# Attention probabilities transposed by VectorE blocks and two DMAs instead of on TensorE, in a four-layer graph network on one core

## Chip, cores and metric

The kernel runs on one core of a Trainium2 chip. The metric is the device time of one execution in microseconds, the median of the timed runs.

## What is computed

The input `x` holds 32 samples of 256 tokens with 384 features, `adj` a 256x256 Boolean graph for each sample. Four residual layers follow one another, each closed by a LayerNorm. The first is a graph attention layer with 12 heads (GAT), which the change leaves alone. The other three are masked self-attention with 6 heads of 64 features:

```python
q = _heads(x @ Wq + bq); k = _heads(x @ Wk + bk); v = _heads(x @ Wv + bv)
scores = jnp.einsum('bhqd,bhkd->bhqk', q, k) / np.sqrt(HEAD_SIZE)
bias = jnp.where(adj, 0.0, -9e15)[:, None]
probs = jax.nn.softmax(scores + bias, axis=-1)
ctx = jnp.einsum('bhqk,bhkd->bhqd', probs, v)      # back to (token, 384)
x = _layernorm(x + ctx @ Wf + bf)
```

All of it is float32 in and out.

## The kernel before

The three attention layers have 96 samples to work through (32 in each), and do so as a software pipeline of slots. A function `slot(cur, nxt, prev, ...)` is written out for each engine. In one slot the engine works on three samples: `nxt` is projected (transposed x, then Q and K in three chunks, then V), `cur` gets its scores and softmax, and `prev` gets its contexts, its output projection ("back") and its LayerNorm. Nothing reorders this: each engine takes its instructions in the order in which its `slot` writes them, and semaphores join the engines. A sample is written `(half, u)`, and `before` and `after` use the same two halves of double buffers by `u`.

A product of two matrices is made of three matmuls (`product`, L78 to L80), with each operand split into a high and a low part in float32r. ScalarE makes the high part out of PSUM (`high_xt`, `high_qk`, `high_ct`), VectorE the low one (`low_xt`, `low_qk`, `low_ct`).

The softmax of a head goes this way. `pair_of_scores` writes the scores of heads 2c and 2c+1 (pair c, three pairs a sample) into the PSUM banks `s0` and `s1`. VectorE's `mask_and_max` (L1001) adds the mask and takes the maximum, ScalarE's `exp` (L727) takes the exponential and its sum, VectorE's `normalise` takes the reciprocal of the sums (L1019) and multiplies the probabilities by it (L1022). The tile `probs` has room for four heads, that is two pairs. TensorE's `pair_of_transposes` (L1411) then turns each 128x128 block of a head, eight blocks a pair, into the PSUM banks `pt0` and `pt1`; ScalarE copies the even head to SBUF (`even_pt`) and VectorE the odd one (`odd_pt`, L1009). The contexts (L1429) multiply V by the turned probabilities `pt_copy`.

GpSimd has the work around it: `make_mask` (L495), `add_output_bias` (L501), the inverse standard deviation (L506, L508) and the LayerNorm itself (L516), and in 12 slots of layers 1 and 2 one part of the next layer's weights split in two (L523, L525). SyncE issues every DMA, in one order: `move` (rows of Q and K to the other half of the partitions, two DMAs of 128 KB a chunk, `stack<-split`), the load of a later sample with its graph (448 KB) and the store of a finished one (384 KB). An instruction that waits on SyncE or GpSimd holds back everything written behind it.

The scratch banks in PSUM are two (`pj0`, `pj1`) for the projections, and one each (`cx`, `pj2`, `pj0`) for the three pairs of contexts.

Of the kernel before, what the change touches and what calls it, by code (L numbers as in the profile page):

```python
# [4 lines left out]
F32 = mybir.dt.float32  # L5
# [63 lines left out]

def held(eng, sem, value, passed):  # L70

    eng.wait_ge(sem, value)
    eng.sem_inc(passed, 1)
# [9 lines left out]
def network(nc, x, adj, gat_w, gat_sd, gat_b, gat_hb, att_w, att_b_col, att_b_row, ident_dram, sel_dram, y):  # L83


    g_STEPS, STEPS = 9, 7
# [3 lines left out]
    g_PT_BUFS, PT_BUFS = 2 * g_QUAD, 6  # L90
    Q, K, V, O = range(4)
    with ExitStack() as ctx:  # L92
# [60 lines left out]
        pt_sb = sb("pt_copy", [P, PT_BUFS, NT, N])  # L153
# [21 lines left out]
        w_lo.append(sb("w_lo1", [P, 4, DC, D], F32R))  # L175
        s_ps = [ctx.enter_context(nc.psum_tensor(f"s{i}", [P, NT, N], F32)) for i in range(2)]
# [3 lines left out]
        cx_banks = [cx_ps, pj_ps[2], pj_ps[0]]  # L180
# [30 lines left out]
        pj_made = sem("pj_made")  # L211
# [5 lines left out]
        inverted, normed = sem("inverted"), sem("normed")  # L217
        transposed = sem("transposed")
        pt_even_read, pt_odd_read = sem("pt_even_read"), sem("pt_odd_read")
        pt_read = [pt_even_read, pt_odd_read]  # L220
# [35 lines left out]
        X, QK, VS = (0, 1), (2, 4, 6), (3, 5)  # L256
        HI_STEPS = len(X) + len(QK)
        BANK_ORDER = ("x0", "x1", "ctx2", "qk0", "v0", "qk1", "v1", "qk2", "back0", "back1")

        def step(half, u, k):  # L260

            return at(STEPS, half, u, k + 1)
# [5 lines left out]
        def bank(u, what):  # L268


            return pj_ps[BANK_ORDER.index(what) % 2]

        def evictions(half, u, h):

            return at(HEADS // 2, half, u, h // 2 + 1)

        def pt_slot(u, h):
            return (HEADS * u + h) % PT_BUFS
# [30 lines left out]
        g_even, g_odd = (HALVES - 1, 0), (HALVES - 1, 1)  # L309

# [3 lines left out]
        def _(sp):  # L314
# [35 lines left out]

            def sample(half, u, stored_pair, loaded_pair):

                move(half, u, 0)
                if stored_pair is not None:
                    store(half - 2 + u, stored_pair, 1 - u)
                move(half, u, 1)
                move(half, u, 2)
                if loaded_pair is not None:
                    load_again(half, u, loaded_pair)
# [17 lines left out]
            start(sp, *g_stored, *stored, *moved)  # L377
# [35 lines left out]
            end = LAYERS * HALVES - 1  # L413
            store(end - 1, HALVES - 2, 1)
# [1161 lines left out]
```

## Time and profile before

| | us |
|---|---|
| median of 3 runs | 2952.93 |
| lowest and highest | 2952.66, 2953.56 |
| span of the profiled execution | 2950.5 |

| engine | busy us | share of the span | instructions |
|---|---|---|---|
| TensorE matmul | 2901.4 | 98% | 22432 |
| TensorE weight load | 2635.8 | 89% | 22432 |
| VectorE | 2593.1 | 88% | 8649 |
| ScalarE | 2428.1 | 82% | 6888 |
| GpSimd | 1269.5 | 43% | 1262 |

The profiled execution is 2.4 us shorter than the median. The GAT layer takes about the first 850 us of the span, the three attention layers the rest. Busy shares tell how full an engine is; what sets the time is read from who waits. Matmuls are pipelined, so the time of one is longer than the distance between two.

### The profile page before, as it was taken

The page shows a single profiled execution, that of the slowest core. Times are in us where ns is not written, and L with a number is a line of the kernel's source. Part 1 is how long each engine was busy: PE and PEld are TensorE (multiplying, and loading weights), DVE is VectorE, ACT ScalarE, POOL GpSimd, SP SyncE. Part 2 cuts the span into 40 slices and gives each one's busy share as a digit, 9 for nine tenths or more (in the row PEclk, how much of TensorE's full clock was granted, in tenths as well). Part 3 has the DMA queues.
Part 4 walks back from the last instruction along what each step waited for, and adds up shares of the span by engine and source line. Part 5 has one row for each costly group of instructions (what it writes and reads, how often), then busy time and mean ns, then how long its engine had stood idle before and what let it go on. Part 6 is the DMA issues. An engine that isn't in the chain of part 4 may idle for free. (4 is left out here: it accounts for less than half of the span.)

```text
span 2950.5 us, 72423 instructions
## 1 busy us (share of the span) xinstructions
PE 2901.4 (98%) x22432; PEld 2635.8 (89%) x22432; DVE 2593.1 (88%) x8649; ACT 2428.1 (82%) x6888; POOL 1269.5 (43%) x1262
## 2 busy tenths in 40 slices
PE   8999999999999999999999999999999999999998
PEld 7888888888889999999999999999999999999997
DVE  6999899999888888888888888888888888888887
ACT  7999999999987777777777777777777777777775
POOL 3777776766643343332332333433323323223233
PEclk9999999999999999999999999999999999999999
DMA  2111111010123222223223222222232222222321
GB/s 91 36 36 36 36 36 36 31 36 31 36 73 110 73 77 77 75 74 81 72 77 109 78 77 75 74 78 74 75 80 77 78 73 77 77 75 75 81 72 55
DMA packets 153211, 198.76 MB, mean 67 GB/s; under 512 B 48896, under 2 KB 115328, under 8 KB 152448
## 3 DMA queue, kind: packets, MB, share of 16 engines
q1 hardware_dynamic: 152832, 194.13, 24.0%
q8 instruction: 186, 3.05, 0.4%
q14 instruction: 193, 1.58, 0.2%
HBM read 68.24 MB, written 50.33 MB: 40 GB/s over the span
## 5 line engine op out<-in xcount | busy, mean ns | idle before, releaser
L501 POOL TENSOR_TENSOR residual<-x,br 128x384 f32<-128x384 f32 x192 | 189.6, 1008 | 1329.4 <-DVE mix L1031 1316.2
L727 ACT ACTIVATE probs<-logits,nmax 128x256 f32<-128x256 f32 x1152 | 574.0, 502 | 111.0 <-DVE nmax L1001 104.1
L78 PE MATMUL pj<-xt_hi,w_lo 128*128 128x256 f32 x1728 | 506.9, 293 | 0.0
L80 PE MATMUL pj<-xt_hi,w_hi 128*128 128x256 f32 x1728 | 480.9, 278 | 0.0
L79 PE MATMUL pj<-xt_lo,w_hi 128*128 128x256 f32 x1728 | 480.8, 278 | 0.0
L1001 DVE CUSTOM_DVE_ANT_0 logits<-s,mask 128x256 f32<-128x256 f32 x1152 | 432.5, 419 | 5.8
L1022 DVE TENSOR_SCALAR probs<-probs,recs 128x256 f32<-128x256 f32 x1152 | 398.3, 387 | 20.4
L598 ACT ACTIVATE g_exps<-g_v,g_nmax 128x256 f32<-128x256 f32 x768 | 385.1, 514 | 2.5 <-DVE g_nmax L907 0.4
L712 ACT ACTIVATE split<-pj,bc 128x256 fp32r<-128x256 f32 x576 | 241.9, 472 | 158.9 <-PE pj L80 158.9
L720 ACT ACTIVATE stack<-split 64x512 fp32r<-64x512 f32 x576 | 361.9, 628 | 8.7
L78 PEld LDWEIGHTS pj<-xt_hi,w_lo 128*128 128x128 f32 x1728 | 324.2, 188 | 49.2 <-issue 36.6
L516 POOL TENSOR_SCALAR out<-mix,mv,rstd 128x384 f32<-128x384 f32 x192 | 317.2, 1660 | 19.9 <-issue 19.3
L79 PEld LDWEIGHTS pj<-xt_lo,w_hi 128*128 128x128 f32 x1728 | 325.2, 188 | 0.0
L80 PEld LDWEIGHTS pj<-xt_hi,w_hi 128*128 128x128 f32 x1728 | 324.0, 187 | 0.0
L907 DVE CUSTOM_DVE_ANT_0 g_v<-s,g_v 128x256 f32<-128x256 f32 x768 | 286.9, 420 | 35.7 <-ACT g_v L592 29.1
L1411 PE MATMUL pt<-identity,probs 128*128 128x128 f32 x2304 | 299.4, 273 | 5.5 <-DVE probs L1022 5.5
L1400 PE MATMUL s<-k_lo,stack 128*128 128x256 f32 x1152 | 297.3, 291 | 0.8 <-DVE nmax L1001 0.7
L1401 PE MATMUL s<-stack 128*128 128x256 f32 x1152 | 288.9, 283 | 0.0
L1411 PEld LDWEIGHTS pt<-identity,probs 128*128 128x128 f32 x2304 | 270.3, 141 | 15.4 <-DVE probs L1022 6.2
L991 DVE SCALAR_TENSOR_TENSOR k_lo<-pj,bc,split 64x256 fp32r<-64x256 f32 x576 | 275.7, 479 | 4.1
L1400 PEld LDWEIGHTS s<-k_lo,stack 128*128 128x128 f32 x1152 | 220.4, 191 | 1.5 <-DVE nmax L1001 1.5
L1401 PEld LDWEIGHTS s<-stack 128*128 128x128 f32 x1152 | 221.4, 192 | 0.0
(122 smaller groups left out, 8094.3 us busy)
## 6 DMA issues: line engine op xcount, KB each, us to landing
stack<-split SPq DMA_DIRECT2D x576, 128.0 KB, 2.3
y<-out SPq DMA_DIRECT2D x128, 384.0 KB, 2.7
x<-y SPq DMA_DIRECT2D x96, 384.0 KB, 3.1
x<-x SPq DMA_DIRECT2D x32, 384.0 KB, 3.1
adj<-adj SPq DMA_DIRECT2D x128, 64.0 KB, 3.0
w_whole<-att_w SPq DMA_DIRECT2D x3, 2304.0 KB, 11.5
g_w_stage<-gat_w SPq DMA_DIRECT2D x2, 576.0 KB, 5.9
br<-att_b_row SPq DMA_DIRECT2D x3, 192.0 KB, 6.1
```

The costliest lines, as they stand in the source:

```text
L78: pe.matmul(out, a[1], b[0], start=first, stop=False)
L79: pe.matmul(out, a[0], b[1], start=False, stop=False)
L80: return pe.matmul(out, a[0], b[0], start=False, stop=last)
L516: pool.tensor_scalar(out_sb[u][:, t, :], mix[:, t, :], mv[:, t, 0:1], rstd[:, t:t + 1], ALU.subtract, ALU.mult).then_inc(ln_done, 1)
L598: last = act.activation(g_exps[:, h % 4, t, :], g_v_sb[:, h % 3, t, :], ACT.Exp, scale=-1.0, bias=g_nmax[:, u, h, t:t + 1], accum_out=g_su ...
L720: last = act.activation(stack[rows_of(s), c, s, :, :], f32(split_slot(u, c)[rows_of(s), K_HI:Q_HI + 1:2, :]), ACT.Identity)
L727: last = act.activation(probs[:, (HEADS * u + h) % 4, t, :], logits[:, h % 2, t, :], ACT.Exp, scale=-1.0, bias=nmax[:, u, h, t:t + 1], acc ...
L1001: last = dve.tensor_tensor_reduce(out=logits[:, h % 2, t, :], in0=s_ps[h % 2][:, t, :], in1=mask[u][:, t, :], scale=-HEAD_DIM ** -0.5, sca ...
L1022: last = dve.tensor_scalar(probs[:, (HEADS * u + h) % 4, t, :], probs[:, (HEADS * u + h) % 4, t, :], recs[:, u, h, t:t + 1], None, ALU.mult)
L1400: pe.matmul(s_ps[s][:, t, :], queries, k_lo[:, c, s, :], start=True, stop=False)
L1401: last = pe.matmul(s_ps[s][:, t, :], queries, stack[:, c, s, STACK_K, :], start=False, stop=True)
L1411: last = pe.transpose(pt_ps[h % 2][:, kt, t * P:(t + 1) * P], probs[:, i, t, kt * P:(kt + 1) * P], ident[:, :])
```

## The change

The transposes leave TensorE. In their place a pair of heads goes this way:

- VectorE's `invert` takes the reciprocals of a pair's sums, and GpSimd's new `normalise` multiplies the pair, 1024 elements a partition, in one instruction. It is written at three places of GpSimd's slot; the LayerNorm of a sample now stands between the first two, one slot later than before (`old`, the sample before `prev`).
- VectorE's `turn` transposes 32x32 blocks with two instructions a pair (512 elements a partition each). It reads `probs` as `p k (h t) r` from `(r k)` with k = 4: within an instruction the innermost step `r` goes over 32 elements that lie 4 elements, 16 bytes, apart.
- SyncE's `lay` writes the turned pair to DRAM (512 KB, 4 KB a partition in one run), `fetch` waits for that and reads it back (512 KB in runs of 1 KB) into `pt_copy`. Each pair has its own `fetched` semaphore, and two buffers `turned_sb` alternate.
- The contexts of `prev` stand later in TensorE's slot, after the second chunk of Q and K of `nxt` and before the third pair of scores of `cur`. They read `pt_copy` as moving operand in runs of 32 elements. `even_pt` and `odd_pt` are gone.
- The projections have three PSUM banks in turn instead of two, and the contexts take `cx` and the two banks that the transposes used. `add_back(old, 1)` and the statistics move to the start of VectorE's next slot.

The diff, cut to its core (`normalise` is GpSimd's, `turn` VectorE's, `slot` and `transpose_x` TensorE's):

```diff
+def before(sample):
+    if sample is None or sample == (0, 0):
+        return None
+    half, u = sample
+    return (half, 0) if u else (half - 1, 1)
...
-        pt_sb = sb("pt_copy", [P, PT_BUFS, NT, N])
+        pt_sb = sb("pt_copy", [P, DC, BLOCKS, RUN])
+        turned_sb = [sb(f"turned_sb{b}", [P, BLOCKS, RUN]) for b in range(2)]
-        cx_banks = [cx_ps, pj_ps[2], pj_ps[0]]
+        cx_banks = [cx_ps[:, 0:N], pt_ps[0][:, 0, :], pt_ps[1][:, 0, :]]
...
+        FIRST_ORDER = ("x0", "x1", "none", "qk0", "v0", "qk1", "v1", "qk2")
+        BANK_ORDER = ("x0", "x1", "qk0", "qk1", "v0", "v1", "qk2", "back0", "back1")
+        def bank(half, what):
+            if half == 0 and what in FIRST_ORDER:
+                return pj_ps[FIRST_ORDER.index(what) % 2]
+            return pj_ps[BANK_ORDER.index(what) % 3]
...
+            def lay(half, u, c):
+                b = turn_buffer(u, c)
+                held(sp, turned, turns(half, u, c), passed)
+                sp.wait_ge(fetched[c], fetches(half, u) - 16)
+                sp.dma_start(turned_dram[c].rearrange("b (r k) n -> (b r) (k n)", k=BLOCKS),
+                             turned_sb[b][:, :, :].rearrange("p k n -> p (k n)")).then_inc(laid[b], 16)
+            def fetch(half, u, c):
+                sp.wait_ge(laid[turn_buffer(u, c)], landings(half, u, c))
+                held(sp, contexts, at(DC, half, u, c + 1 - DC), passed)
+                sp.dma_start(pt_sb[:, c, :, :], turned_dram[c].rearrange("b p n -> p b n")).then_inc(fetched[c], 16)
...
+            def normalise(half, u, c):
+                b = turn_buffer(u, c)
+                heads = slice(2 * b, 2 * b + 2)
+                held(pool, inverted, turns(half, u, c), passed)
+                pool.tensor_tensor(probs[:, heads, :, :].rearrange("p h t n -> p (h t) n"), probs[:, heads, :, :].rearrange("p h t n -> p (h t) n"),
+                                   recs[:, u, 2 * c:2 * c + 2, :].rearrange("p h t -> p (h t)").unsqueeze(2).to_broadcast([P, 2 * NT, N]),
+                                   ALU.mult).then_inc(normed, 1)
...
-                act.wait_ge(transposed, at(HEADS, half, u, h - 3))
+                act.wait_ge(turned, turns(half, u, h // 2 - 2))
...
+            def turn(half, u, c):
+                b = turn_buffer(u, c)
+                dve.wait_ge(normed, turns(half, u, c))
+                dve.wait_ge(laid[b], landings(half, u, c) - 16)
+                for kt in range(NT):
+                    last = dve.transpose(
+                        turned_sb[b][:, :, :].rearrange("p k (z h q) -> p k z h q", z=NT, h=2 * NT)[:, :, kt],
+                        probs[:, 2 * b:2 * b + 2, :, kt * P:(kt + 1) * P].rearrange("p h t (r k) -> p k (h t) r", k=BLOCKS))
+                last.then_inc(turned, 1)
...
             def slot(cur, nxt, prev, layers, opening=False, part=None):
-                if prev:
-                    pair_of_transposes(*prev, 2)
                 if nxt:
                     transpose_x(*nxt, 0, opening)
                     transpose_x(*nxt, 1, opening)
                 if cur:
                     pair_of_scores(*cur, 0)
-                if prev:
-                    pair_of_contexts(*prev, 0, nxt)
-                    pair_of_contexts(*prev, 1, nxt)
-                    pair_of_contexts(*prev, 2, nxt)
                 if nxt:
                     make_qk(*nxt, 0, nxt_layer)
                 if cur:
                     pair_of_scores(*cur, 1)
                 if nxt:
-                    make_v(*nxt, 0, nxt_layer, prev)
-                if cur:
-                    pair_of_transposes(*cur, 0)
-                if nxt:
                     make_qk(*nxt, 1, nxt_layer)
+                if prev:
+                    pair_of_contexts(*prev, 0)
+                    pair_of_contexts(*prev, 1)
+                    pair_of_contexts(*prev, 2)
                 if cur:
                     pair_of_scores(*cur, 2)
                 if nxt:
+                    make_v(*nxt, 0, nxt_layer)
                     make_v(*nxt, 1, nxt_layer)
                     make_qk(*nxt, 2, nxt_layer)
                 if prev:
                     make_back(*prev, 0, nxt, prev_layer)
-                if cur:
-                    pair_of_transposes(*cur, 1)
-                if prev:
                     make_back(*prev, 1, nxt, prev_layer)
...
+            def transpose_x(half, u, t, opening):
+                if half or opening:
                     pe.wait_ge(pj_read, at(HI_STEPS, half, u, 0))
+                if t == 1:
+                    pe.wait_ge(back_read, at(NT, half, u, 1 - 3 * NT))
```

VectorE, the end of a steady slot before, from the third chunk of Q and K of `nxt` (`split`, `k_lo`) to the start of the next slot (`xt_lo`):

```order
L988 SCALAR_TENSOR_TENSOR split<-pj,bc,split 128x256 [waits scores,pj_hi]
L991 SCALAR_TENSOR_TENSOR k_lo<-pj,bc,split 64x256 x2
L1019 RECIPROCAL recs<-sums 128x2 [waits exped]
L1022 TENSOR_SCALAR probs<-probs,recs 128x256 [waits inverted]
L1022 TENSOR_SCALAR probs<-probs,recs 128x256
L1009 COPY pt_copy<-pt 128x512 [waits contexts,transposed]
L1031 TENSOR_TENSOR mix<-pj,residual 128x384 [waits back_made,ln_done,x_biased] x2
```

The same place now, from the low parts of the contexts (`ct_lo`):

```order
L1073 SCALAR_TENSOR_TENSOR ct_lo<-pt,bc,ct_hi 128x256 [waits ct_hi_done] x2
L1087 STREAM_TRANSPOSE turned_sb<-probs 128x4x128 [waits laid1,normed]
L1087 STREAM_TRANSPOSE turned_sb<-probs 128x4x128
L1079 RECIPROCAL recs<-sums 128x4 [waits exped]
L1087 STREAM_TRANSPOSE turned_sb<-probs 128x4x128 [waits laid0,normed]
L1087 STREAM_TRANSPOSE turned_sb<-probs 128x4x128
L1053 SCALAR_TENSOR_TENSOR split<-pj,bc,split 128x256 [waits scores,pj_hi]
L1056 SCALAR_TENSOR_TENSOR k_lo<-pj,bc,split 64x256 x2
L1098 TENSOR_TENSOR mix<-pj,residual 128x384 [waits back_made,ln_done,x_biased] x2
```

Two turned pairs now stand ahead of the last chunk's low part, with the reciprocal of the third pair between them.

GpSimd, one steady slot before, from the bias of one slot to that of the next:

```order
L501 TENSOR_TENSOR residual<-x,br 128x384
L506 TENSOR_SCALAR var<-mv 128x2 [waits aggr]
L508 TENSOR_TENSOR rstd<-var,half_neg 128x2 [waits var_eps]
L516 TENSOR_SCALAR out<-mix,mv,rstd 128x384 [waits stored0,rstd_done]
L516 TENSOR_SCALAR out<-mix,mv,rstd 128x384
L495 TENSOR_SCALAR mask<-adj 128x512 [waits maxed,x_loaded1]
L501 TENSOR_TENSOR residual<-x,br 128x384 [waits back_read,pj_made]
```

And now:

```order
L557 TENSOR_TENSOR residual<-x,br 128x384
L579 TENSOR_TENSOR probs<-probs,recs 128x1024 [waits inverted]
L562 TENSOR_SCALAR var<-mv 128x2 [waits aggr]
L564 TENSOR_TENSOR rstd<-var,half_neg 128x2 [waits var_eps]
L572 TENSOR_SCALAR out<-mix,mv,rstd 128x384 [waits stored0,rstd_done]
L572 TENSOR_SCALAR out<-mix,mv,rstd 128x384
L579 TENSOR_TENSOR probs<-probs,recs 128x1024 [waits inverted]
L551 TENSOR_SCALAR mask<-adj 128x512 [waits maxed,x_loaded1]
L579 TENSOR_TENSOR probs<-probs,recs 128x1024 [waits inverted]
L557 TENSOR_TENSOR residual<-x,br 128x384 [waits back_read,pj_made]
```

The three products of a slot stand before the LayerNorm, behind it, and behind the mask.

SyncE, one steady slot before:

```order
L349 DMA stack<-split 64x512
L330 DMA y<-out 128x2x384 [waits ln_done]
L349 DMA stack<-split 64x512 [waits pj_read,scores]
L349 DMA stack<-split 64x512
L349 DMA stack<-split 64x512 [waits pj_read,scores]
L349 DMA stack<-split 64x512
L325 DMA x<-y 128x2x384 [waits x_biased]
```

And now, from the second `move` on:

```order
L374 DMA stack<-split 64x512
L388 DMA pt_copy<-turned 128x4x256 [waits laid0,contexts]
L355 DMA y<-out 128x2x384 [waits ln_done]
L381 DMA turned<-turned_sb 128x1024 [waits turned,fetched1]
L388 DMA pt_copy<-turned 128x4x256 [waits laid1,contexts]
L381 DMA turned<-turned_sb 128x1024 [waits turned,fetched2]
L374 DMA stack<-split 64x512 [waits pj_read,scores]
L374 DMA stack<-split 64x512
L388 DMA pt_copy<-turned 128x4x256 [waits laid0,contexts]
L350 DMA x<-y 128x2x384 [waits x_biased]
```

The last `move` now stands behind two writes to DRAM and one read, each with a wait of its own.

## Rows read from the trace of the kernel before

**Rows 1.** The page: busy time by engine, DMA share in 40 slices.

```profile
PE 2901.4 (98%) x22432; PEld 2635.8 (89%) x22432; DVE 2593.1 (88%) x8649; ACT 2428.1 (82%) x6888; POOL 1269.5 (43%) x1262
...
DMA  2111111010123222223223222222232222222321
```

**Rows 2.** The page's groups: busy us, mean ns | idle before, releaser.

```profile
L1022 DVE TENSOR_SCALAR probs<-probs,recs 128x256 f32<-128x256 f32 x1152 | 398.3, 387 | 20.4
...
L1411 PE MATMUL pt<-identity,probs 128*128 128x128 f32 x2304 | 299.4, 273 | 5.5 <-DVE probs L1022 5.5
```

**Rows 3.** Waits, 1200 to 2800 us: who for whom, total us, times, longest.

```profile
POOL residual L501 <- DVE mix L1031: 1025.0, 72, 14.9
```

**Rows 4.** Timeline of TensorE in a steady slot and two later: start us, us, what.

```profile
2001.73 0.39 PE L78 MATMUL pj<-xt_hi,w_lo 128*128 128x256 f32 x1
...
2003.96 0.28 PE L1400 MATMUL s<-k_lo,stack 128*128 128x256 f32 x1
...
2006.48 1.04 PE L1411 MATMUL pt<-identity,probs 128*128 128x128 f32 x8
2007.28 0.36 PE L78 MATMUL pj<-xt_hi,w_lo 128*128 128x256 f32 x1
...
2019.17 0.82 PE L1347 MATMUL pj<-identity,x 128*128 128x128 f32 x6
...
2020.88 1.08 PE L1429 MATMUL cx<-pt_copy,v 128*64 128x256 f32 x8
...
2895.10 0.82 PE L1347 MATMUL pj<-identity,x 128*128 128x128 f32 x6
```

**Rows 5.** Timeline of VectorE in the same slot.

```profile
2005.05 0.47 DVE L988 SCALAR_TENSOR_TENSOR split<-pj,bc,split 128x256 fp32r<-128x256 f32 x1
...
2006.45 0.42 DVE L1001 CUSTOM_DVE_ANT_0 logits<-s,mask 128x256 f32<-128x256 f32 x1
...
2006.80 0.42 DVE L1001 CUSTOM_DVE_ANT_0 logits<-s,mask 128x256 f32<-128x256 f32 x1
...
2019.07 1.01 DVE L1036 BATCH_NORM_STATS2 stats<-mix 128x6 f32<-128x384 f32 x2
...
2020.33 0.53 DVE L982 TENSOR_TENSOR xt_lo<-pj,xt_hi 128x384 fp32r<-128x384 f32 x1
2020.77 0.68 DVE L1009 COPY pt_copy<-pt 128x512 f32<-128x512 f32 x1
2021.37 0.55 DVE L982 TENSOR_TENSOR xt_lo<-pj,xt_hi 128x384 fp32r<-128x384 f32 x1
```

**Rows 6.** Timeline of ScalarE: a head's exponential starts, and the next work.

```profile
2001.36 0.50 ACT L727 ACTIVATE probs<-logits,nmax 128x256 f32<-128x256 f32 x1
...
2002.34 0.46 ACT L739 ACTIVATE ct_hi<-pj,bc 128x256 fp32r<-128x256 f32 x1
```

**Rows 7.** GpSimd's groups of the whole run, by line.

```profile
L441 POOL TENSOR_TENSOR g_z_right<-g_s_dst,g_sel 128x512 fp32r<-128x512 f32 x192 | 193.4, 1047 | 21.2 <-DVE g_s_dst L869 21.2
L501 POOL TENSOR_TENSOR residual<-x,br 128x384 f32<-128x384 f32 x192 | 189.6, 1008 | 1329.4 <-DVE mix L1031 1316.2 <-PE pj L1347 13.2
...
L459 POOL TENSOR_TENSOR mix<-mix,residual 128x768 f32<-128x768 f32 x32 | 59.2, 1850 | 146.1 <-DVE mix L894 146.1
...
L525 POOL TENSOR_TENSOR w_lo<-w_whole,w_hi 128x384 fp32r<-128x384 f32 x36 | 36.8, 1021 | 6.7 <-POOL w_hi L523 6.7
```

**Rows 8.** Timeline of GpSimd: from the variance to the mask of one slot.

```profile
2897.30 0.23 POOL L506 TENSOR_SCALAR var<-mv 128x2 f32<-128x2 f32 x1
...
2901.92 0.62 POOL L495 TENSOR_SCALAR mask<-adj 128x512 f32<-128x512 uint8 x1
```

**Rows 9.** The page's DMA issues: KB each, median us from issue to landing.

```profile
y<-out SPq DMA_DIRECT2D x128, 384.0 KB, 2.7
x<-y SPq DMA_DIRECT2D x96, 384.0 KB, 3.1
...
w_whole<-att_w SPq DMA_DIRECT2D x3, 2304.0 KB, 11.5
```

More of the change, by code:

```diff
@@ L413, in _ @@
             end = LAYERS * HALVES - 1
+            lay(end, 1, 0)
+            fetch(end, 1, 0)
             store(end - 1, HALVES - 2, 1)
+            lay(end, 1, 1)
+            fetch(end, 1, 1)
+            lay(end, 1, 2)
+            fetch(end, 1, 2)
             store(end, HALVES - 1, 0)
@@ L1346, in transpose_x @@
                 for c in range(DC):
-                    last = pe.transpose(bank(u, f"x{t}")[:, c * P:(c + 1) * P], x_sb[u][:, t, c * P:(c + 1) * P], ident[:, :])
+                    last = pe.transpose(bank(half, f"x{t}")[:, c * P:(c + 1) * P], x_sb[u][:, t, c * P:(c + 1) * P], ident[:, :])
                 last.then_inc(pj_made, 1)
@@ L1352, in make_qk @@
                     pe.wait_ge(w_split, weights_split(layer))
-                pe.wait_ge(pj_read, split_of(half, u, X[1] if chunk == 0 else QK[chunk - 1]))
+                    pe.wait_ge(pj_read, split_of(half, u, X[1]))
+                    pe.wait_ge(back_read, at(NT, half, u, 2 - 3 * NT))
+                elif half == 0 or chunk == 2:
+                    pe.wait_ge(pj_read, split_of(half, u, QK[chunk - 1]))
                 hi, lo = w_hi[layer % 2], w_lo[layer % 2]
@@ L1369, in make_v @@
                 for c in range(DC):
[L1370 removed]
+                    last = product(pe, bank(half, f"v{t}")[:, 0:D], (xt_hi[:, c, rows], xt_lo[:, c, rows]), (hi[:, V, c, :], lo[:, V, c, :]),
                                    first=c == 0, last=c == DC - 1)
[L1372 removed]
+                last.then_inc(v_made, 1)
             def make_back(half, u, t, nxt, layer):
@@ L1376, in make_back @@
                     pe.wait_ge(ct_split, at(DC, half, u, DC))
-                if nxt and t == 0:
-                    pe.wait_ge(v_read, at(NT, *nxt, NT))
-                elif nxt:
-                    pe.wait_ge(pj_read, split_of(*nxt, QK[2]))
-                elif t == 0:
-                    pe.wait_ge(back_read, at(NT, half, u, 0))
+                if nxt:
+                    pe.wait_ge(v_read, at(NT, *nxt, t + 1))
+                else:
+                    pe.wait_ge(back_read, at(NT, half, u, t + 1 - NT))
                 hi, lo = w_hi[layer % 2], w_lo[layer % 2]
@@ L1385, in make_back @@
                 for c in range(DC):
-                    last = product(pe, bank(u, f"back{t}")[:, 0:D], (ct_hi[u][:, c, rows], ct_lo[u][:, c, rows]), (hi[:, O, c, :], lo[:, O, c, :]),
+                    last = product(pe, bank(half, f"back{t}")[:, 0:D], (ct_hi[u][:, c, rows], ct_lo[u][:, c, rows]), (hi[:, O, c, :], lo[:, O, c, :]),
                                    first=c == 0, last=c == DC - 1)
```

278 lines of the change are left out of this document (135 added, 143 removed).

## Prediction, made before the changed kernel had run

> **What bounds the kernel now.** I read the busy shares first: TensorE 98% [rows 1]. Then the waits: in 73 slots the only long one is GpSimd's, for the last step of VectorE [rows 3], and nobody waits for GpSimd there. Then TensorE's timeline, which has no gap worth a name: each group starts where the one before lets go [rows 4]. So the three attention layers run at TensorE's pace. The same step, the first transposes of x, stands at 2019.17 and at 2895.10, 40 slots apart [rows 4]: a slot takes 21.90 us. Everything below is counted in this slot, of which some 94 are alike. The sum is made against the span of 2950.5; the median lies 2.4 above it.
>
> **What is removed.** TensorE gives back three groups of eight transposes a slot, 2304 in all [rows 2]. One group holds the array from 2006.48 to 2007.28 [rows 4]: 0.8 us, and 0.9 for the others, 2.6 a slot. TensorE alone would then go at 19.3. The order now puts the first chunk of Q and K right behind the transposes of x and one pair of scores, and it needs the low part of x, which comes about 2.1 after the slot's start; before, contexts covered that. It costs 0.4, so TensorE's floor is 19.7. VectorE loses twelve scalings (0.39 us each [rows 2]) and three copies of 0.60, the distance from 2020.77 to 2021.37 [rows 5]; ScalarE loses three copies. If nothing else held, the gain would be 2.2 a slot, 207 us. The question is what is late next.
>
> **What is added, and its price.**
> GpSimd's product over 1024 elements. Dense tensor_tensor takes 1008 ns for 384 elements and 1850 for 768 [rows 7]: 2.19 ns each and 0.17 fixed, so 2.4 us. The one that reads a broadcast operand takes 1047 for 512 [rows 7], 1.71 ns each: 1.9 us. The new one is of this second kind. I take N = 2.0 and keep 1.9 to 2.4.
>
> VectorE's turn. No row shows a block transpose. The nearest is the copy of 512 elements, one every 0.60 [rows 5]: a pair of turns would be T = 1.2 to 1.3. That copy reads its elements side by side, the turn reads every fourth one; GpSimd's two rates for the same arithmetic [rows 7] show that an engine's time an element depends on how its operands lie. As upper end I take two passes of the copy for each, T = 2.4, and a bit for the start of each, 2.7. Between these ends I choose T = 2.2, near the two passes, because all 512 elements of the instruction are apart and none of the copy's are. This is a choice, and the forecast hangs on it.
>
> The DMAs. A load of 384 KB lands after 3.1, a store after 2.7; the load of 2304 KB takes 11.5, so 8.4 us for the 1920 KB more, 0.56 for 128 KB [rows 9]. A lay of 512 KB is then about 3.3 and a fetch 3.7, 7.0 together.
>
> **The new chain.** I go through a slot, from TensorE's first transpose of x at 0. The low part of x is done at 2.1. VectorE takes a head's maximum in two instructions 0.35 apart (2006.45, 2006.80 [rows 5]), 0.7 a head: two heads at 3.5. ScalarE's exponentials take 0.98 a head (2001.36 to 2002.34 [rows 6]) and end at 5.0. VectorE's statistics (1.3, from 2019.07 to 2020.33 [rows 5]) fit meanwhile. The reciprocal ends at 5.2. From there two strands run.
>
> VectorE's strand: maxima of the second pair to 6.6, low part of the first chunk 1.4 (2005.05 to 2006.45 [rows 5]) to 8.0, turn 0 to 8.0+T, reciprocal 0.2, second chunk 1.4, maxima 1.4, three low parts of contexts 1.25 (each like the first instruction of 2005.05, 0.4), so 12.25+T; turn 1; reciprocal 0.2; then it must wait for GpSimd's third product, N+0.1, since the reciprocal of pair 2 stands behind turn 1; turn 2; the third chunk's low part 1.4. The next slot's first transpose waits for that (`pj_read`). Sum: 12.25 + T + T + 0.2 + 2.1 + T + 1.5 = 16.1 + 3T.
>
> GpSimd's strand: product 0 from 5.3 to 7.3, then variance, deviation and LayerNorm, 4.6 from 2897.30 to the mask at 2901.92 [rows 8], product 1 to 14.0, turn 1 cannot start before, so 14.0 + T + 0.3 + N + T + 1.5 = 17.9 + 2T. It decides only where T is below 1.8.
>
> With T = 2.2 the slot is 22.7, with 1.3 it is 20.5, and break-even with 21.90 lies at T = 1.93, 0.97 us for one instruction. What was idle before at VectorE becomes a strand in which TensorE waits 3 us a slot, before the transposes of x.
>
> **The sum.** 22.7 - 21.9 = 0.8, by 94 slots 75. At the end the last sample's probabilities go through lay and fetch (7.0) and product, less the transposes, of which the empty last slot hides a little: about +8. At the passage from GAT I give 5 for DMAs and products in a stretch not written for them. 2950.5 + 75 + 13 = 3038.5, and 2.4 for the median: **3041 us**.
>
> **What hides the DMAs.** SyncE issues lay 2 when turn 2 ends, 1.5 before the slot's end; `move` 2 is behind it. Lay lands 1.8 into the next slot, fetch about 5.5. TensorE wants pair 2 at 9.1 (transposes of x and scores 1.7, from 2019.17 to 2020.88; two chunks of 2.2, from 2001.73 to 2003.96 [rows 4]; scores 1.0; the wait of 0.4; two pairs of contexts 1.8). Slack: 3.6. If lay and fetch take over 10.6 together it is gone, and each us beyond costs 94. For the volume: six times 512 KB at 0.56 for 128 KB is 13.4 us a slot, and the transfers there now fill 2 to 3 tenths of the engines [rows 1], 5 to 6 us. That is 19 of 22.7, room but little.
>
> **A rule that speaks against the change.** The turn's read steps 16 bytes each element. The Trainium skill ("Vector Engine (DVE) Microarchitecture Reference", 5.2 Measured stream behaviour on trn2) says that a port streams at full rate only in runs of at least two adjacent words; a source that hops at every element cost 1.73 ns an element there, a small step up to 2.5. By that page a turn instruction would be, as an estimate, 0.96 to 1.36 us, and the slot 21.9 to 24.2. No row of this trace reads this way, so it neither agrees nor differs. The page's "one source" case ran at full rate in one layout, so it leaves the fast case open.
>
> **The rivals.**
> Rival A, turn as quick as a copy. T = 1.2 to 1.5. For it: one source, one result an element, as in the copy [rows 5]. Against: the step. GpSimd's strand rules, slot 20.5. In 24 slots a part of the weights is split ahead of product 2 (1.02 [rows 7] and half that for the cast) and adds about 0.9. So -1.4 by 94, +20, +10 for the two ends: 2848, and **2851** as a median; 2825 to 2885 with N at its ends. The change is faster here.
>
> Rival B, turn at one and a half copies. T = 1.7 to 1.95, slot 21.2 to 21.95, times 2900 to 2970, middle **2940**. The removed transposes are paid back almost to the last us. Half of it and a bit lie below 2947.
>
> Rival C, heavier than two copies, or the DMAs bind. T = 2.7 gives 24.2, +216+13, **3182**. The DMA form: fetch's pieces are 1 KB against 1.5 KB of the loads [rows 9]; if lay and fetch together take 12 us in the crowd, contexts of pair 2 are late, the scores behind them too, and the slot grows by 1.4 over 22.7, again near 3170. Against: the slack of 3.6.
>
> That the change does not do what it says: TensorE's transposes are gone by the order, and no copy takes their place, so I give that nothing.
>
> **Chances.** Forecast (T 2.0 to 2.5, slot 22.1 to 23.6, 2985 to 3126) 0.42; A 0.29; B 0.17; C 0.12. Faster by over 0.2% (below 2947): 0.29 + 0.08 = 0.37. Within 0.2%, which is about what a measurement of this kernel can tell from no change: 0.05. Slower: 0.04 + 0.42 + 0.12 = 0.58. Both signs hold much, so the range must reach into A and stops short of most of C: **2835 to 3130**. The forecast's own range is 2985 to 3126.
>
> **What would show it.** The turn's mean duration decides: about 1.1 us for the forecast, 0.6 to 0.7 for A, 0.9 to 1.0 for B. TensorE's idle time should stand before the transposes of x, released by VectorE's `k_lo`, some 3 us a slot; GpSimd's product should read 1.9 to 2.1; VectorE should be at about 90% of the span. A TensorE wait before the contexts would say that the DMAs bind and the chain is wrong. The granted clock is to stay full through gaps of 3 us; were it to fall, all TensorE groups would be slower and the sum too small. A slot of 19.7 would say that I invented both strands.

## The result and the profile after

The changed kernel takes 3057.56 us, median of 4 runs (3051.53 to 3063.40); the kernel before takes 2952.80 on the same chip (4 runs, 2952.37 to 2953.56). The ratio is 1.0353, with a 95% interval of 1.0339 to 1.0368: 3.5% slower. The forecast was 3041, so it lies 17 us under the measured time, and the range held it.

The page of the kernel after: busy time by engine, then the groups (busy us, mean ns | idle before, releaser), then DMA issues.

```profile
PE 2771.7 (91%) x20128; PEld 2479.0 (81%) x20128; DVE 2587.4 (85%) x7497; ACT 2272.8 (75%) x6600; POOL 1809.7 (59%) x1550
...
L579 POOL TENSOR_TENSOR probs<-probs,recs 128x1024 f32<-128x1024 f32 x288 | 545.5, 1894 | 461.7 <-DVE recs L1079 461.7
...
L1087 DVE STREAM_TRANSPOSE turned_sb<-probs 128x512 f32<-128x512 f32 x576 | 609.8, 1099 | 205.2 <-POOL probs L579 202.3
...
L1411 PE MATMUL pj<-identity,x 128*128 128x128 f32 x576 | 114.9, 316 | 202.3 <-DVE k_lo L1056 191.7
...
turned<-turned_sb SPq DMA_DIRECT2D x288, 512.0 KB, 4.0
pt_copy<-turned SPq DMA_DIRECT2D x288, 512.0 KB, 4.3
```

TensorE went from 98% [rows 1] to 91%, in a longer span. The two new operations have their prices here: a half turn is 1.099 us, a product 1.894. VectorE is as busy as before, 2587 against 2593 us: 576 half turns cost 610, about what 1152 scalings (398 [rows 2]) and the copies had cost. The last group answers to the transposes of x, which had no gap ahead of them [rows 4]; now TensorE stands idle for 192 us in front of them, released by VectorE's low part `k_lo`.

Waits of the kernel after, 1200 to 2800 us: who for whom, total us, times, longest.

```profile
POOL probs L579 <- DVE recs L1079: 342.8, 141, 5.0
...
DVE turned_sb L1087 <- POOL probs L579: 150.2, 71, 2.4
PE pj L1411 <- DVE k_lo L1056: 142.4, 71, 2.3
```

Among them are two that [rows 3] did not have and that fit together: once a slot VectorE waits 2.1 us for GpSimd, and once a slot TensorE waits 2.0 us for VectorE. The timeline of VectorE at the end of a slot shows the chain (start us, us, what):

```profile
1993.66 2.10 DVE L1087 STREAM_TRANSPOSE turned_sb<-probs 128x512 f32<-128x512 f32 x2
1995.68 0.13 DVE L1079 RECIPROCAL recs<-sums 128x4 f32<-128x4 f32 x1
1997.92 2.06 DVE L1087 STREAM_TRANSPOSE turned_sb<-probs 128x512 f32<-128x512 f32 x2 [2.11 <-POOL probs L579]
1999.90 0.45 DVE L1053 SCALAR_TENSOR_TENSOR split<-pj,bc,split 128x256 fp32r<-128x256 f32 x1
2000.26 0.97 DVE L1056 SCALAR_TENSOR_TENSOR k_lo<-pj,bc,split 64x256 fp32r<-64x256 f32 x2
```

Turn 1, reciprocal 2, the wait for product 2, turn 2, the low part of chunk 2; then TensorE starts, here in TensorE's timeline, with the starts of the third and of the last transposes that the readings use:

```profile
2001.28 1.55 PE L1411 MATMUL pj<-identity,x 128*128 128x128 f32 x6 [2.01 <-DVE k_lo L1056]
...
2024.29 1.20 PE L1411 MATMUL pj<-identity,x 128*128 128x128 f32 x6 [2.00 <-DVE k_lo L1056]
...
2047.46 1.20 PE L1411 MATMUL pj<-identity,x 128*128 128x128 f32 x6 [2.02 <-DVE k_lo L1056]
...
2069.50 1.20 PE L1411 MATMUL pj<-identity,x 128*128 128x128 f32 x6 [1.59 <-DVE k_lo L1056]
...
2887.89 1.20 PE L1411 MATMUL pj<-identity,x 128*128 128x128 f32 x6 [2.02 <-DVE k_lo L1056]
```

The last of these is the 39th after the first, so a slot takes 22.73 us on average. But the slots are not alike: they take 23.01, 23.17 and 22.04, and this pattern of three goes on to the end with few breaks, one of them right behind the lines shown. The windows of the same stretch show why (columns: us, busy of PE, PEld, DVE, ACT, POOL with counts, granted clock, DMA share, GB/s):

```profile
2001.28:2005.00 3.72, 3.69 (x18) 3.38 (x19) 3.04 (x9) 1.31 (x3) 1.97 (x2) 0.54 0.85 319
2005.00:2024.28 19.28, 17.29 (x128) 15.72 (x127) 16.27 (x46) 14.05 (x41) 10.50 (x8) 1.00 0.56 181
2024.29:2026.00 1.71, 1.58 (x10) 1.37 (x11) 1.55 (x3) 0.97 (x2) 0.57 (x1) 0.85 0.48 78
2026.00:2028.00 2.00, 2.00 (x12) 2.00 (x11) 1.93 (x8) 0.69 (x4) 1.41 (x2) 0.50 0.97 353
...
2047.46:2069.50 22.04, 19.89 (x144) 17.73 (x144) 19.22 (x54) 15.36 (x43) 12.49 (x10) 1.00 0.71 219
```

After the idle 2.0 us the granted clock falls in two slots of three (50 of the 78 between 1200 and 2960 us) to its lower level (0.50 of full, 1.2 GHz) for 3.4 us: almost at once in the first slot, about 1 us later in the second, not at all in the third. In the third the chain alone shows: 22.04. The other two pay about 1.0 more, since the second pair of scores comes late and VectorE waits for it, as a further line of the same waits says:

```profile
DVE logits L1066 <- PE s L1466: 41.8, 48, 1.8
```

In the kernel before, the clock is full in all of these slots.

### The profile page after: what moved, and what is told of

It reads as the page before. It is cut to its first block and busy times, and to the rows that moved or that the text cites. A ratio compares the mean times of both kernels' runs of the same rounds, so it can differ in the third digit from the quotient of the medians.

```text
span 3049.7 us, 67047 instructions
## 1 busy us (share of the span) xinstructions
PE 2771.7 (91%) x20128; PEld 2479.0 (81%) x20128; DVE 2587.4 (85%) x7497; ACT 2272.8 (75%) x6600; POOL 1809.7 (59%) x1550
## 5 line engine op out<-in xcount | busy, mean ns | idle before, releaser
L579 POOL TENSOR_TENSOR probs<-probs,recs 128x1024 f32<-128x1024 f32 x288 | 545.5, 1894 | 461.7 <-DVE recs L1079 461.7
L1087 DVE STREAM_TRANSPOSE turned_sb<-probs 128x512 f32<-128x512 f32 x576 | 609.8, 1099 | 205.2 <-POOL probs L579 202.3
L87 PE MATMUL pj<-xt_lo,w_hi 128*128 128x256 f32 x1728 | 500.2, 289 | 0.0
L86 PEld LDWEIGHTS pj<-xt_hi,w_lo 128*128 128x128 f32 x1728 | 349.7, 202 | 20.3 <-issue 18.2
L785 ACT ACTIVATE xt_hi<-pj 128x384 fp32r<-128x384 f32 x192 | 94.4, 491 | 357.4 <-PE pj L1411 357.2
L87 PEld LDWEIGHTS pj<-xt_lo,w_hi 128*128 128x128 f32 x1728 | 345.1, 200 | 0.0
L1465 PE MATMUL s<-k_lo,stack 128*128 128x256 f32 x1152 | 341.6, 323 | 3.5 <-DVE nmax L1066 3.5
L1466 PE MATMUL s<-stack 128*128 128x256 f32 x1152 | 324.1, 308 | 0.0
L1411 PE MATMUL pj<-identity,x 128*128 128x128 f32 x576 | 114.9, 316 | 202.3 <-DVE k_lo L1056 191.7
L1465 PEld LDWEIGHTS s<-k_lo,stack 128*128 128x128 f32 x1152 | 245.0, 213 | 40.3 <-issue 36.5
```

The costliest lines, as they stand in the source:

```text
L86: pe.matmul(out, a[1], b[0], start=first, stop=False)
L87: pe.matmul(out, a[0], b[1], start=False, stop=False)
L579: pool.tensor_tensor(probs[:, heads, :, :].rearrange("p h t n -> p (h t) n"), probs[:, heads, :, :].rearrange("p h t n -> p (h t) n"), rec ...
L1087: last = dve.transpose(turned_sb[b][:, :, :].rearrange("p k (z h q) -> p k z h q", z=NT, h=2 * NT)[:, :, kt], probs[:, 2 * b:2 * b + 2, :, ...
L1465: pe.matmul(s_ps[s][:, t, :], queries, k_lo[:, c, s, :], start=True, stop=False)
L1466: last = pe.matmul(s_ps[s][:, t, :], queries, stack[:, c, s, STACK_K, :], start=False, stop=True)
```

## The experiments

Times are medians of 4 runs (10 in experiment 10), each with runs of the kernel before on the same chip, which stood between 2952.8 and 2953.7 for all of them. "Gain" is against the 3057.6 of the kernel after; one us a slot is 94 us.

**1. Dense turn, keys ordered by TensorE's operands.**

```diff
-  probs[...].rearrange("p h t (r k) -> p k (h t) r", k=BLOCKS)
+  probs[...].rearrange("p h t (k r) -> p k (h t) r", k=BLOCKS)
-  pe.matmul(s_ps[s][:, t, :], queries, k_lo[:, c, s, :], ...)
+  pe.matmul(apart(s_ps[s][:, t, :]), queries, keys(k_lo[:, c, s, :]), ...)   # "p (t r k) -> p t k r"; the stack's K and the mask alike
```

> The turn reads four dense runs of 32 keys instead of every fourth key. To keep the keys in their places the scores' moving operands (k_lo and the stack's K) and the mask are read in the order in which the turn's blocks want them, so what is computed is the same. Theory (chain): a slot is the chain of VectorE from turn 1 over invert 2, GpSimd's product 2 and turn 2 to the next x transposes, so each turn enters three times; its 1.10 us per half comes from reading elements 16 bytes apart. Dense, a half should take 0.6 to 0.7 us (the copies of before: 0.6), a pair 1.2 to 1.4 instead of 2.1: 23.0 - 3 * 0.8 = 20.6, with the wait of 2.1 us for product 2 kept, bounded below by TensorE's 19.7: 2950 of span after - 94 * 2.4 = 2820 to 2860 us. Rival 1 (the form does not matter, a block transpose costs by its elements): a half stays at 1.10, time unchanged at 3057. Rival 2 (the DMAs set the slot): halves fall but the wait of SyncE grows by as much, 3040 to 3060. Rival 3 (GpSimd's product or strand sets it): gain of at most one turn per slot, 94 * 0.8 = 75, about 2980. TensorE's strided moving reads may cost something: its matmuls for scores should stay at their pace of 0.118 us.

2997.7 us (ratio 1.015, 1.0134 to 1.0165). The turn did what was expected, the total did not. The groups of this kernel:

```profile
L1097 DVE STREAM_TRANSPOSE turned_sb<-probs 128x512 f32<-128x512 f32 x576 | 374.9, 689 | 208.3 <-POOL probs L589 198.7
L1475 PE MATMUL s<-k_lo,stack 128*128 128x256 f32 x1152 | 491.5, 427 | 1.0 <-DVE nmax L1076 1.0
```

A half turn takes 0.689 instead of 1.099. But the scores' matmuls, whose moving operand is now read 16 bytes apart, start every 0.23 us (TensorE's timeline of this kernel, start and length) instead of every 0.12:

```profile
2000.59 0.43 PE L1475 MATMUL s<-k_lo,stack 128*128 128x256 f32 x1
2000.82 0.43 PE L1476 MATMUL s<-stack 128*128 128x256 f32 x1
2001.06 0.43 PE L1475 MATMUL s<-k_lo,stack 128*128 128x256 f32 x1
```

For 24 a slot that is 2.8 us, so TensorE's own work goes from the forecast's 19.3 to 22.1, and the slots measure 22.1, nearly all alike. TensorE is busy for 1591 of 1600 us. The edit moved the fault from VectorE to TensorE. It gave the turn's price, but its total says nothing on the chain.

**2. The low part of chunk 2 ahead of turn 2.**

```diff
   turn(*cur, 1)
   invert(*cur, 2)
-  turn(*cur, 2)
   low_qk(*nxt, 2, nxt_layer)
+  turn(*cur, 2)
```

> Only VectorE's order in a slot is changed: the low part of Q and K of chunk 2 for the next sample stands between invert 2 and turn 2 instead of behind turn 2. TensorE's x transposes wait for that low part, so they no longer wait for product 2 and turn 2. Theory (chain): the 1.0 us low part fills part of the 2.1 us wait for GpSimd's product, and TensorE's 2.0 us gap before the transposes goes, and with it the half clock of the first 3.7 us of a slot (1.1 us): the slot falls from 23.0 by 1.0 (filled wait) to 3.0, to between 20.0 and 22.0; point 20.8, that is 3057 - 94 * 2.2 = 2850. Rival 1 (VectorE's volume binds, 19 us plus waits that only move): at most 1.0 per slot, 2960. Rival 2 (DMAs bind): turn 2 ends later by up to 1.0, so its lay, its fetch and the contexts of pair 2 come later; if they bind, time unchanged or slower, 3050 to 3100.

2984.6 us (1.0107, 1.0092 to 1.0122): a gain of 73, less than half of the 207 expected. The direction is right and rival 1 fits better. The waits of this kernel, 1200 to 2800 us, tell what held:

```profile
PE pj L1412 <- DVE mix L1098: 118.8, 72, 2.2
```

The second group of x transposes writes a bank that the first residual sum must have left, and this sum still stood behind turn 2: TensorE waits 1.65 a slot. I had removed one of two waits for the same group. Its slots take 21.4 or about 22.9. Windows over a short slot, and over 3.4 us of the long one behind it:

```profile
2190.70:2212.00 21.30, 19.39 (x145) 17.76 (x144) 19.38 (x54) 15.24 (x43) 12.49 (x10) 1.00 0.71 226
...
2216.00:2219.40 3.40, 3.40 (x17) 3.40 (x18) 2.54 (x13) 2.08 (x8) 1.02 (x2) 0.50 0.47 154
```

27 of the 29 long slots hold such a stretch at half clock, about 4 us behind their start, and no short one does; what lengthened the other two is open. So the order took 0.7 off a slot at full clock (22.1 to 21.4), and the clock still cost about 1.5 in every long one.

**3. Both edits.**

> Both edits: the dense turn (keys put in place by the scores' operands and the mask) and the low part of chunk 2 ahead of turn 2. Theory (chain): nothing of the turn is left ahead of the x transposes, and the slot comes to TensorE's own floor of 19.7 to 20.0 us: 3057 - 94 * (23.0 - 19.9) = 2766, between 2750 and 2820; TensorE's gap before its transposes below 0.3 us and its clock full in all of the slot. Rival (DMAs or GpSimd bind at 20.5 or more): no better than the better of the two single edits, 2830 or more, with a wait of TensorE for the fetched turn or of VectorE for the product.

3069.3 us (1.0391, 1.0374 to 1.0408). A clear miss, slower than either edit. The waits:

```profile
DVE split L1063 <- ACT split L802: 194.0, 71, 2.8
```

TensorE, slowed by its strided reads, makes chunk 2 late. With its low part in front, turn 2 and the residual sum stand behind a wait of up to 2.8 us that turn 2 used to fill. An order that fits a VectorE-bound slot is wrong in a TensorE-bound one.

**4. Matmuls in the gap.**

```diff
   make_back(*prev, 1, nxt, prev_layer)
+  if prev and nxt:
+      for i in range(14):
+          pe.matmul(pt_ps[0][:, 1, :], g_ident_r[:, :], g_s_dst[0][:, :], start=True, stop=True)
```

> 14 matmuls whose result nobody reads stand on TensorE behind the last of the sample's back product, in the 2.0 us gap ahead of the x transposes; nothing else is changed. Theory (the idle 2.0 us makes the clock fall to half for the next 3.7 us, and that costs 1.1 us of each slot): the granted clock of the slot's start is full, its matmuls keep 0.118 us, the slot falls from 23.0 to 21.9 to 22.2, 3057 - 94 * 0.9 = 2970 (2950 to 2990). Rival (the clock's fall is absorbed, since VectorE sets the slot anyway): clock full, time within 10 us of 3057. Rival 2 (the fillers are in the way of the transposes): slower, up to 3057 + 94 * 0.3 = 3085.

3002.8 us (1.0169, 1.0153 to 1.0184), gain 55. The window from the transposes on, beside that of the kernel after (0.54):

```profile
2001.00:2004.70 3.70, 3.29 (x25) 2.91 (x26) 3.49 (x13) 1.66 (x5) 1.99 (x2) 1.00 0.94 322
```

Apart from the passage between two layers the clock is full in every slot, and nearly all slots measure 22.1 to 22.2, as the one in three of the kernel after. So the lower clock costs 0.58 a slot on average. I had expected 0.9 because I took the slot of 23.0 for all of them. The remaining idle time ahead of the transposes is 0.4, and the slot is no longer than without the fillers: VectorE still sets it.

**5. A quarter of what the DMAs move.**

```diff
-  sp.dma_start(turned_dram[c].rearrange("b (r k) n -> (b r) (k n)", k=BLOCKS), turned_sb[b][...])
+  sp.dma_start(turned_dram[c, 0], turned_sb[b][:, 0, :])
-  sp.dma_start(pt_sb[:, c, :, :], turned_dram[c].rearrange("b p n -> p b n"))
+  sp.dma_start(pt_sb[:, c, 0, :], turned_dram[c, 0])
```

> The lay and the fetch of a pair each move one block of the four (128 KB instead of 512 KB), and the contexts read that one block four times, by as many matmuls of the same size as before; three quarters of what the turn moves is left out, so the contexts are not those of the reference. Nothing else is changed, so the volume of the two DMAs goes from 1.0 MB to a quarter per pair. Theory (the DMAs are hidden: fetch 2 has 2.6 us to spare): time within 10 us of 3057. Rival (DMAs bind, or their traffic slows what else moves, the stack's moves of K and Q among them): 3 pairs of 1.5 to 3 us fewer, if they all stood on the path, down to 2850; anything below 3035 says they count.

3047.5 us (1.0317, 1.0299 to 1.0334), a gain of 10, the edge of what "hidden" allowed. The landings fall to 1.7 and 2.2 us, the wait of TensorE ahead of x stays (143.4 us, 71 times), and the slots keep their pattern of three. The DMAs don't bind the kernel after.

**6. Half of GpSimd's product.**

```diff
-  heads = slice(2 * b, 2 * b + 2)
+  heads = slice(2 * b, 2 * b + 1)
```

> GpSimd normalises one head of each pair (512 elements per partition instead of 1024); the other head is left unnormalised. All else stays. Theory (product 2 stands once in the chain between VectorE's invert 2 and turn 2): the product falls from 1.89 to about 1.0 us, VectorE's wait for product 2 from 2.1 to 1.2 us, the slot by 0.9 or a little more, since TensorE's gap shrinks too: 3057 - 94 * 0.9 = 2973, 2955 to 2985. Rival (GpSimd's own strand binds, three products per slot): -2.7 per slot, 2805 to 2850. Rival (GpSimd is covered): 3050 to 3060.

2936.9 us (0.9944, 0.993 to 0.9959), a gain of 121, or 1.28 a slot; 0.9 was expected.

```profile
L579 POOL TENSOR_TENSOR probs<-probs,recs 128x512 f32<-128x512 f32 x288 | 299.8, 1041 | 578.5 <-DVE recs L1079 578.5
```

The product is 0.85 shorter, and the slots measure 21.3: 0.8 less than the 22.1 at full clock. So the product enters the chain once. The other 0.5 is the clock: TensorE's gap shrinks to 1.05 us, and the granted clock stays at 1.00. My expectation had left it out.

**7. The dense turn by itself.** The change to `turn` of experiment 1 alone; nothing puts the keys back in V's order.

> The turn alone reads dense runs of 32 keys; the scores, the mask and both DMAs stay as in the kernel after, so the keys reach the contexts in another order than V's rows, and the attention's sums pair the wrong keys with V: only the time is of use. Every other operation has the size and form of the kernel after. In the first experiment the half of a turn took 0.69 us dense instead of 1.10, but the scores' matmuls, which read their moving operand 16 bytes apart, went from 0.30 to 0.43 us each and took most of it back. Theory (chain, three turns in it): a pair takes 1.30 instead of 2.1, 3 * 0.8 = 2.4 us less per slot: 23.0 to 20.6, 3057 - 94 * 2.4 = 2830, 2800 to 2865. Rival (only turn 2 in the chain counts, as the other two lie in slack): -0.8 per slot and the clock's part, 2950 to 2985. Rival (form does not count without the other edits): 3050.

2897.5 us (0.9813, 0.9798 to 0.9827): a gain of 160, 1.70 a slot, between the theory's 2.4 and the rival's 0.8. The slots scatter, mostly from 20.1 to 22.3, and three reach 24.3 to 24.8: in these the clock falls for 3.4 us, some 12 to 14 us behind their start. Waits and a DMA issue of this kernel:

```profile
PEld pt L1478 <- issue: 78.5, 72, 4.1
...
turned<-turned_sb SPq DMA_DIRECT2D x288, 512.0 KB, 5.2
```

TensorE now waits up to 4.1 us ahead of the contexts, which take what the fetch brings, and a lay lands after 5.2 instead of 4.0. The wait that the prediction had named as the sign of binding DMAs appears once the chain is short.

**8. The first residual sum, too, ahead of turn 2.**

```diff
   low_qk(*nxt, 2, nxt_layer)
-  turn(*cur, 2)
   add_back(*prev, 0)
+  turn(*cur, 2)
```

> VectorE's order again, a step further than in the second experiment: behind invert 2 stand the low part of chunk 2, the first residual sum of the previous sample, and only then turn 2, so that neither TensorE's x transposes nor the banks that they write wait for turn 2, and turn 2 lies in the time in which VectorE waits for the transposes and ScalarE's high parts of x. Theory (in the second experiment x transposes waited 119 us in 72 slots for the sum behind turn 2): that wait of 1.65 us goes, the slot falls from 22.3 by 1.0 to 2.0, 2985 - 94 * 1.5 = 2845, 2800 to 2890. Rival 1 (fetch 2 comes later, as turn 2 ends about 1 us later, and the contexts of pair 2 wait for it): gain under 0.5 per slot, 2940 to 2990, with a wait of TensorE for the fetch in its place. Rival 2 (VectorE's own queue: turn 2 ahead of the low parts of x holds those up by as much as it saves): 2950 to 3000.

2913.6 us (0.9873, 0.9854 to 0.9892), gain 144. This kernel computes the whole reference and is 1.3% faster than the kernel before, with the turn at its 1.1 us. The x transposes wait for nothing, most slots are 20.92, and the clock is full. The wait has moved on:

```profile
PE pj L86 <- DVE xt_lo L1047: 120.0, 75, 1.6
```

TensorE waits 1.6 a slot for the low part of x, since turn 2 stands ahead of it. Against experiment 2 that is 0.76 a slot, less than the 1.0 to 2.0 expected, as 1.6 of waiting went at one place and came back, partly covered, at the next. The slot at full clock fell by 0.5 (21.4 to 20.9), and the falls of the clock are gone besides.

**9. That order, the dense turn, keys ordered by ScalarE.**

```diff
-  act.activation(probs[..., t, :], logits[:, h % 2, t, :], ACT.Exp, ...)
+  act.activation(probs[..., t, :].rearrange("p (z k r) -> p z r k", ...), logits[...].rearrange("p (z r k) -> p z r k", ...), ACT.Exp, ...)
```

> The order of the eighth kernel of this study (low part of chunk 2 and first residual sum ahead of turn 2), with the dense turn, and with the keys put in their places by ScalarE: the exponential reads logits in order and writes the probabilities with the keys of a 128-wide tile in the order in which the dense turn wants them, so what is computed is the same, and TensorE's operands stay dense. Theory (each turn still enters: turns 1 and 2 by 0.8 us each at most, since the order edit took turn 2 off the x transposes but it still stood ahead of the low parts of x, with TensorE waiting 1.6 us for these): slot 21.5 falls to 20.3 to 20.9, 2914 - 94 * 0.9 = 2830, 2800 to 2870. Rival 1 (the fetch binds now, as TensorE's contexts waited up to 4.1 us for it in the dense kernel): no gain over the order alone or over the dense turn alone, 2880 to 2915. Rival 2 (the exponential's strided write is slow, over 0.1 us for each 256 elements above its 0.50): 12 of them per slot, 1.2 us or more back, in the strand max, exp, invert: 2880 to 2950.

2895.9 us (0.981, 0.9791 to 0.9829), the fastest kernel here that computes the whole reference, 1.9% faster than the kernel before; but only 18 under experiment 8, and both rivals came true.

```profile
L807 ACT ACTIVATE probs<-logits,nmax 128x256 f32<-128x256 f32 x1152 | 744.4, 758 | 207.8 <-DVE nmax L1066 205.2
...
PEld pt L1479 <- issue: 76.7, 61, 4.5
```

The exponential that writes 16 bytes apart takes 758 ns, dense 499, and TensorE waits for the fetch as in experiment 7. Which of the two costs more was not separated.

**10. The same, keys ordered by the lay.**

```diff
-  sp.dma_start(turned_dram[c].rearrange("b (r k) n -> (b r) (k n)", k=BLOCKS), turned_sb[b][...])
+  for g in range(BLOCKS):
+      sp.dma_start(turned_dram[c, g].rearrange("(k r) n -> r k n", k=BLOCKS), turned_sb[b][g * 32:(g + 1) * 32, :, :])
```

> The order of the eighth kernel and the dense turn, as in the ninth, but the keys are put in their places by the lay: it is written as four DMAs of 32 partitions and 128 KB each, in runs of 1 KB instead of 4 KB; ScalarE's exponential is dense again and what is computed is the same. Theory (the ninth kernel lost 0.26 us per exponential, 12 per slot, partly in its critical strand, and waited for the fetch besides): with the exponential at 0.50 us the slot is bounded by the fetch alone, at or a little under the dense kernel's 21.2; 2850 to 2895, point 2875. Rival 1 (SyncE's queue: four issues at 0.33 us or more in place of one, 9 more per slot, push the fetches and the stack's moves back by 1 us each): 2900 to 2980. Rival 2 (the exponential was the ninth kernel's bound and the fetch not): 2820 to 2850.

2954.6 us (1.0001, 0.9987 to 1.0015), in the range of rival 1. SyncE's queue, start us and us:

```profile
2003.10 0.38 SPq L389 DMA_DIRECT2D pt_copy<-turned  x1
2003.59 2.05 SPq L382 DMA_DIRECT2D turned<-turned_sb  x4
2005.82 1.20 SPq L374 DMA_DIRECT2D stack<-split  x2
```

Four issues take 2.05 us here, 2.5 and 3.1 at the other two lays of the slot, where one takes 0.33 to 0.5. A move of K and Q stands right behind two of the three lays and a fetch behind the third. That this queue alone costs the 59 us against experiment 9 was not separated: the lay's pieces are 1 KB besides, and ten slots of 23.6 to 24.5 hold a fall of the clock, where experiment 9 has four such. Ordering the keys thus had a price on each of the three engines tried: 2.8 us a slot on TensorE, 0.26 us an exponential on ScalarE, 1.6 us or more a lay in SyncE's queue.

**11. Dense turn, a quarter of the DMAs.** Experiments 5 and 7 together.

> The dense turn (keys in another order than V's rows, as before) with the lay and the fetch at one block of four, read four times by the contexts: both edits leave out or alter part of the computation, only the time is of use. Theory (with the turn dense, TensorE's contexts waited 78 us in 72 slots, up to 4.1 us, for the fetch: the DMAs had become the bound that cost the dense kernel 0.7 us per slot against its expectation): these waits go, and the slot comes to 20.6, 2897 - 94 * 0.7 = 2830, 2805 to 2865. Rival (that wait was in the shadow of another): within 15 us of 2897.

2808.7 us (0.9507, 0.9491 to 0.9523), 89 under experiment 7, more than the 67 expected. The slots are 20.05 to 20.2, without scatter, except the ones in which GpSimd splits weights: these take 20.87 or 20.88. The wait ahead of the contexts is gone. GpSimd's timeline shows the difference, product 2 behind the split and, a slot later, product 2 that only waits for its reciprocal:

```profile
1878.82 1.02 POOL L589 TENSOR_TENSOR w_lo<-w_whole,w_hi 128x384 fp32r<-128x384 f32 x1 [0.19 <-DVE recs L1078]
1879.80 1.90 POOL L578 TENSOR_TENSOR probs<-probs,recs 128x1024 f32<-128x1024 f32 x1
...
1899.85 1.90 POOL L578 TENSOR_TENSOR probs<-probs,recs 128x1024 f32<-128x1024 f32 x1 [0.91 <-DVE recs L1078]
```

The same edit that gave 10 us with the turn at 1.1 gives 89 with the turn at 0.69: the DMAs are the next bound, right behind the chain. That 0.9 us a slot goes with their volume is shown. With the DMAs out of the way the dense turn is worth 239 us (experiment 5 to 11), 2.5 a slot, of which 0.58 is the clock by experiment 4. Whether it is the landing time or the traffic that holds up the moves is open.

## Why the prediction was right

**The path.** "TensorE's idle time should stand before the transposes of x, released by VectorE's `k_lo`", "a strand in which TensorE waits": both waits are in the trace at the named places, once a slot. Experiment 6 shows that N enters the chain once: 0.85 less product, 0.8 less slot at full clock. For T, take the distance from the start of a pair of turns to the next work, as the prediction did with its copies: 1.98 in the timeline above (1997.92 to 1999.90), 1.23 in the same place of experiment 11 (1901.78 to 1903.01). Slots at full clock fell from 22.1 to 20.1, by 2.0, where three times 0.75 is 2.25. By the prediction's sums VectorE's chain would be 19.7 there, as TensorE's floor, and GpSimd's strand 20.1, so the slot should have passed to GpSimd's strand, and the slots agree: those with a split of weights are longer by 0.8 in experiment 11 (forecast: 0.9) and not in experiment 6 or the kernel after. So the two sums together hold; no run shows the threefold T alone.

**The slot** was forecast at 22.7 and averages 22.73. That this is so exact is chance. With T = 2.0 and N = 1.89 the formula gives 22.0 (3 times 0.2 less, 0.1 less), and the third slots show 22.04 to 22.15. Nearly all of the missing 0.7 is the clock, of which the prediction said: "The granted clock is to stay full through gaps of 3 us; were it to fall, all TensorE groups would be slower and the sum too small". It fell to half after 2.0 us, and experiment 4 prices it at 0.58 a slot, 55 us. This step was wrong; a T and an N chosen a little high covered it.

**T, the deciding choice**, was 1.1 for a half turn, "near the two passes, because all 512 elements of the instruction are apart". Measured: 1.099 a half turn, with 1.0 from one start to the next since they overlap a little, and 0.689 for the dense one, experiment 1. The reason holds, too: the operation is the same, only its step changed. The dense one costs little more than the copy's 0.60 [rows 5], so Rival A was right on the price of a dense turn and wrong on this one. The Trainium skill ("Vector Engine (DVE) Microarchitecture Reference", 5.2 Measured stream behaviour on trn2) has sources that hop pay more for each element. The trace agrees, and the measured 1.099 lies within the estimate of 0.96 to 1.36 made from it.

**N** was 2.0, measured 1.894. Of the two kinds of row at [rows 7], the one with the broadcast operand was the right choice: in experiment 6 the product over 512 takes 1041 ns, where that row has 1047.

**TensorE's gap** was to be 3 us and is 2.0. 22.1 less the floor of 19.7 leaves 2.4; the rest of the forecast's 3 was the 0.6 by which its chain was too long at full clock.

**The DMAs.** Lay 3.3 and fetch 3.7 were forecast, 4.0 and 4.3 measured: together 8.3, so 1.3 more, taken from the slack of 3.6. Experiment 5 confirms that they are hidden there, and Rival C's DMA form is not what happened. The slack was called small in volume, and experiments 7 and 11 show how small: 0.9 us a slot as soon as the slot nears 21.

**The ends.** The sum had 13 us for tail and crossing. 94 times 0.83 is 78 and the span grew by 99.2, so about 21 lie outside the alike slots, 8 more than forecast. The tail has most of it: from the start of the last transposes of x (2895.10 before, [rows 4]; 2979.3 after) to the end of the span it was 55.4 and is 70.4, so 15.0 more, where 8 had been forecast. That leaves 6 for the passages, where 5 had been. With 3 for the slot's 0.03 that is the 11 by which the span of 3049.7 misses 3038.5. The other 5.5 are between the profiled execution and the median, 7.9 here against the 2.4 assumed: the profile is of the quickest of the four runs. What makes the tail longer no run took apart.

**VectorE** was to be at about 90% and is at 85%. The rows of before give nearly that: 2593, less 398 for the scalings and 196 for 288 copies of 0.68 [rows 5], plus 576 half turns of 1.1, is 2633, and 87% of 3041. It shows that an engine may be on the path at a lower share than it had while it was not.

## What to carry to other kernels

When work leaves the engine that bounds, write down for every engine the order of one period and add it up as a chain: here an engine at 85% set the time, because three turns and one foreign product stood in a row ahead of the other's first instruction. Then look at what that instruction really needs. Two lines moved in VectorE's order, without a cheaper operation, made 3.5% slower into 1.3% faster. An order of elements that one engine wants is paid for on another, so price the strided side on each engine before choosing it, and ask which resource is next: the DMAs that were free at a slot of 22.7 cost 0.9 us at 21.

## What the runs showed of the hardware

- TensorE's granted clock fell to its lower level (1.2 GHz) for 3.4 us after a gap of 2.0 us, in two slots of three; the gap ahead of the third was as long (2.02 us). With gaps of 1.05 us (experiment 6) it stayed at 1.00, and with 1.6 behind the transposes and a pair of scores (experiment 8) too, both but for the passage between two layers; with one of 1.65 between the two groups of x transposes (experiment 2) it fell in 27 of 78 slots and was 0.97 on average. So the length of the gap does not decide alone.
- VectorE's block transpose of 512 f32 per partition: 1.099 us when its read steps 16 bytes, 0.689 in runs of 32.
- TensorE's matmul of 256 columns: with a moving operand whose elements lie 16 bytes apart one starts every 0.233 us, with a dense one every 0.118, both at full clock.
- ScalarE's exponential over 256 elements: 0.758 us with a write 16 bytes apart, 0.499 dense.
- A DMA of 512 KB lands after 4.0 to 4.3 us where one of 128 KB takes 1.7 to 2.2, and 5.2 in the crowded slot of experiment 7; stores of 384 KB went from 2.7 [rows 9] to 4.7 beside the new traffic, and back to 2.6 with a quarter of it (experiment 5).
